# Routing tokens to experts: five chunks instead of six, and a new order of the steps inside a chunk

## The reference, cut to what matters

```
x  = x + gnn(...)                       # h of the last batch norm is added
xn = layernorm(layernorm(x))            # the expert block normalises twice
logits = layernorm(x) @ Wr + br         # [6250, 8]
top_p, top_idx = top_k(softmax(logits), 2)
weights = top_p / top_p.sum()
out = sum over the 2 experts of weights * (gelu(xn_e @ W1[e] + b1[e]) @ W2[e] + b2[e])
```

## Time and profile before

| what | us |
|---|---|
| median of three runs (5987.56 to 5988.58) | 5987.89 |
| the profiled execution's own time | 5985.42 |
| its span, first to last instruction | 5983.6 |
| `route()`, first instruction to that of `experts()` | 3373.6 to 3558.6 |
| mean granted TensorE clock, share of full speed | 0.758 |

### The profile page before, as it was taken

One profiled execution on the slowest core, in us unless ns is written; L12 is line 12 of the kernel. 1 busy time (PEld: TensorE's weight loads), 2 busy tenths in 40 slices (PEclk: granted clock), 3 DMA queues, 4 the chain that ended last, 5 costly groups with the idle time before them and its releaser, 6 DMA issues. The chain is left out here.

```text
span 5983.6 us, 101443 instructions
## 1 busy us (share of the span) xinstructions
PE 4448.4 (74%) x24203; PEld 3115.8 (52%) x24204; DVE 3008.1 (50%) x7622; ACT 2469.0 (41%) x6463; POOL 3450.6 (58%) x3585
## 2 busy tenths in 40 slices
PE   5477777767777776667667649999957777777898
PEld 4254545433444443334333449999945555555566
DVE  7544444444444444333333533333358778878745
ACT  0544444434344443333333324444444444444221
POOL 0477777777777776777777452222237776766001
PEclk6577777766666666666666659999978888888899
DMA  4677777767777776777777552222144443333101
GB/s 128 192 198 196 197 197 196 198 183 201 206 201 204 203 201 185 192 196 192 196 192 196 161 181 35 35 37 35 34 145 115 114 108 106 106 106 96 56 1 43
DMA packets 550732, 862.18 MB, mean 144 GB/s; under 512 B 210941, under 2 KB 398326, under 8 KB 550422
## 3 DMA queue, kind: packets, MB, share of 16 engines
q0 software_dynamic: 219840, 641.37, 40.5%
q1 hardware_dynamic: 330710, 218.97, 12.3%
HBM read 709.79 MB, written 150.21 MB: 144 GB/s over the span
## 5 line engine op out<-in xcount | busy, mean ns | idle before, releaser
L1024 POOL DMA_INDIRECT rows<-node_limbs,psrc x2496 | 2366.0, 948 | 832.2 <-issue 567.0
L1299 PE MATMUL ps<-rows,hot 128*128 128x257 bf16 x7488 | 1638.0, 365 | 874.4 <-DMA rows<-node_limbs,psrc 728.6
L1088 DVE TENSOR_TENSOR shared<-shared,ps 128x257 f32 x2496 | 1056.4, 423 | 1639.5 <-PE ps L1299 1332.1
L1299 PEld LDWEIGHTS ps<-rows,hot 128*128 128x128 bf16 x7488 | 772.0, 122 | 1673.4 <-DVE shared L1088 825.4
L2234 POOL DMA_INDIRECT rows<-attn_table,psrc x832 | 789.8, 949 | 385.7 <-issue 222.7
L1213 ACT ACTIVATE away<-iota_f,pdl 128x128 f32<-128x128 f32 x2496 | 759.2, 387 | 46.5 <-PE ps L1299 46.2
L2541 PE MATMUL ps<-rows,hot 128*128 128x264 f32 x1664 | 583.1, 500 | 231.8 <-DVE rows L2335 175.7
L2541 PEld LDWEIGHTS ps<-rows,hot 128*128 128x128 f32 x1664 | 370.8, 239 | 362.1 <-issue 174.0
L1870 POOL DMA_INDIRECT resid<-feat,slot_node x105 | 164.1, 1563 | 622.4 <-DVE feat L1885 619.6
L2356 DVE TENSOR_TENSOR sums<-sums,ps 128x264 f32 x832 | 356.8, 429 | 113.1 <-PE ps L2541 42.5
L1987 PEld LDWEIGHTS ps<-feat 128*128 128x128 f32 x3360 | 393.2, 193 | 8.3 <-DVE feat L1914 2.4
(11 more groups left out here) (466 smaller groups left out, 5298.8 us busy)
## 6 DMA issues: line engine op xcount, KB each, us to landing
slot_rows<-blank SPq DMA_DIRECT2D x450, 130.0 KB
rows<-node_limbs,psrc POOLq DMA_INDIRECT x2496, 3.3
feat<-in_edge_attr_dram SPq DMA_DIRECT2D x832, 32.0 KB
node_limbs<-limbs SPq DMA_DIRECT2D x99, 196.0 KB, 3.9
feat<-slot_rows SPq DMA_DIRECT2D x105, 130.0 KB
rows<-attn_table,psrc POOLq DMA_INDIRECT x832
node_limbs<-limbs SPq DMA_DIRECT2D x12, 784.0 KB, 3.6
w<-in_L_ffn_W_dram SPq DMA_DIRECT2D x8, 1024.0 KB, 11.6
```

The lines of the kernel that those rows point to most:

```text
L1024: g.indirect_dma_start(rows[:, n % RING, :], None, tables[k % 2], bass.IndirectOffsetOnAxis(ap=psrc[:, n:n + 1], axis=0)).then_inc(row_sem ...
L1088: v.tensor_tensor(row, row, ps[banks(k, i)[h * G + b]][:, 0:F + 1], ALU.add).then_inc(added.h, 1)
L1299: mm = pe.matmul(ps[cycle[s]][:, 0:F + 1], hot[:, 2 * half + h, b, :], rows[:, s, m * LIMB:m * LIMB + F + 1], start=(m == 0), stop=(m == 2))
```

## The change: what it does

The chunks become five: 7, 9, 11, 11 and 11 tiles. `picks(n - 1)` follows right after `spreads(n)`, so one chunk later instead of two. `ranks(n - 2)` moves to after the fourth addition of chunk n. ACT normalises four tiles, then does `second(n - 1)`, and stays four tiles ahead of its copies. PE does `rank(n - 2)` after the second tile of a chunk, and awaits the router's weights after the first tile of chunk 1; DVE awaits them before its first picks.

```
-        CHUNKS = [(0, 4), (4, 9), (9, 17), (17, 27), (27, 38), (38, NT)]
+        CHUNKS = [(0, 7), (7, 16), (16, 27), (27, 38), (38, NT)]
+        SOME = 4
 # DVE
-                    v.wait_ge(wr_in.h, 32)
-                    for n in range(len(CHUNKS) + 2):
-                        lo, hi = CHUNKS[n] if n <= LAST else (0, 0)
+                    for n, (lo, hi) in enumerate(CHUNKS):
                         for d in range(lo, hi):
                             add(d)
                             if d > lo:
                                 seen(d - 1)
-                            if n > 1 and d == lo + 4:
-                                picks(n - 2)
-                        if n <= LAST:
-                            seen(hi - 1)
-                            spreads(n)
-                        else:
-                            picks(n - 2)
-                        if n > 1:
-                            ranks(n - 2)
+                            if n > 1 and d == lo + SOME - 1:
+                                ranks(n - 2)
+                        seen(hi - 1)
+                        spreads(n)
+                        if n == 1:
+                            v.wait_ge(wr_in.h, 32)
+                        if n > 0:
+                            picks(n - 1)
+                    ranks(LAST - 1)
+                    picks(LAST)
+                    ranks(LAST)
 # ACT
                         a.wait_ge(scale_ready.h, n + 1)
-                        expert_row(lo)
-                        for e in range(lo + 1, hi):
+                        for e in range(lo, lo + SOME):
                             expert_row(e)
-                            keep(e - 1)
-                            if n > 0 and e == min(lo + 5, hi - 1):
-                                second(n - 1)
-                        keep(hi - 1)
+                        if n > 0:
+                            second(n - 1)
+                        for e in range(lo, hi):
+                            if e + SOME < hi:
+                                expert_row(e + SOME)
+                            keep(e)
 # PE
-                    pe.wait_ge(wr_in.h, 32)
-                    for n in range(len(CHUNKS) + 2):
+                    for n in range(len(CHUNKS) + 1):
 ...
                         for d in range(lo, hi):
                             turn_hidden(d, n)
+                            if n == 1 and d == lo:
+                                pe.wait_ge(wr_in.h, 32)
                             if n > 1 and d == lo:
-                                logit(lo_before - 1, n - 2)
+                                logit(CHUNKS[n - 2][1] - 1, n - 2)
+                            if n > 1 and d == lo + 1:
+                                rank(n - 2)
                             if d - lo >= AHEAD - 1 and before:
                                 z_tile(before.pop(0))
-                            if n > 1 and d == min(lo + 7, hi - 1):
-                                rank(n - 2)
                         if n > LAST:
                             logit(CHUNKS[n - 2][1] - 1, n - 2)
-                            if n > LAST + 1:
+                        for at, e in enumerate(before):
+                            z_tile(e)
+                            if n > LAST and at == 1:
                                 rank(n - 2)
-                        for e in before:
-                            z_tile(e)
-                        if n == LAST + 1:
-                            rank(n - 2)
-                        lo_before = lo
+                    logit(NT - 1, LAST)
+                    rank(LAST)
```

More of the change, by code:

```diff
@@ L1768, in rank @@
                         pe.matmul(of_bank(P), ones[:], by_expert, start=True, stop=True).then_inc(ranked.h, 1)
-                    pe.wait_ge(wr_in.h, 32)
-                    for n in range(len(CHUNKS) + 2):
+                    for n in range(len(CHUNKS) + 1):
                         lo, hi = CHUNKS[n] if n <= LAST else (0, 0)
-                        before = list(range(*CHUNKS[n - 1])) if 0 < n <= LAST + 1 else []
+                        before = list(range(*CHUNKS[n - 1])) if n > 0 else []
                         late = before[:1]
```

## The result

The changed kernel takes 5973.0 us (median of ten runs, 5971.3 to 5978.2) against 5988.8 (ten, 5982.2 to 5992.6): a ratio of 0.9975, 95% interval 0.9967 to 0.9984. Forecast: 5974.7, a ratio of 0.9978. The profiled execution took 5974.99, its span 5973.2.

What follows compares the result with a forecast made beforehand. POOL's scatters, fed in chunks by DVE and PE, bound the stage: third chunk starts at 3458.0, plus 82.4 and 2 x 1.275, ends at 3542.9, 13.2 us less. Median 5987.89 becomes 5974.7, range 5968 to 5981.5.

Steps and rivals of the forecast that it cites:

- last scatter ends: POOL's end of the stage: 3458.0 + 82.4 + 2 x 1.275 = 3542.9, against 3556.1 before.
- What bounds the stage: In the routing stage, POOL alone ends it: 98 scatters need 125 us, plus 20.0 us of waits for slots between chunks.
- The cycle of 22.7 and 23.0: Chain of PE and DVE from one chunk's end of picks to the next: 22.7 or 23.0 us.
- the 0.94 between slots and POOL: For each chunk, POOL begins scattering 0.94 us after its slots are known, read from 3410.36 to 3411.30.
- The table load of Exp: On ACT, Exp with one table load has 2.9 us behind the picks and is in time.
- The moved waits: The two unconditional waits that moved cost nothing: bias row in by 3378 before, both now reached later.
- PE's earlier start: PE no longer stands 12.0 us for the bias row; it waits for `affine(0)` and begins at 3375.9.
- the low level: PE's granted clock in the chunks taken as 0.50 (1.2 GHz), giving a step of 1.60 us a tile.
- Rival 1: PE at 2.4 GHz in the chunks, DVE sets a cycle of 20.1: 19.7 us less, 5968.2; chance 0.15.
- Rival 2: Two cycles 3 us longer each, from instruction gaps and ACT's copy: 7 us less than before, 5981; chance 0.17.
- Rival 3: `logit` always late, PE's step 2.4 instead of 1.60: end 4 us later than before, 5992; chance 0.06.
- The sum: Whole stage: last scatter's end from 3556.1 to 3542.9, 13.2 us less.

Runs made afterwards that it cites:

- the table of four kernels: Kernel before, its five new chunks only, its new order only, and the changed kernel: last scatter ends 182.5, 178.9, 172.2 and 169.3 us after ACT's first `affine`.
- the third chip: The changed kernel measured again, unaltered, on a chip where the kernel before takes 6832.4 us: 6833.7 us, ratio 1.0002.
- the filled kernel: The changed kernel with PE's idle stretches filled with 26 and 18 transposes that nobody reads: 5970.3 us, ratio 0.9970 to the kernel before.
- even chunks: The changed kernel with six chunks of 7, 7, 8, 8, 9 and 10 tiles: 6819.1 us on the third chip, ratio 0.9980 to the kernel before.

## Why the prediction was right

Step by step, forecast and measured (absolute positions; the stage began 0.26 us earlier in the changed kernel's execution):

| step | forecast | measured |
|---|---|---|
| first addition | 3376.6 | 3376.32 |
| `picks(0)`, `(1)`, `(2)` end | 3404.9, 3427.6, 3450.6 | 3404.86, 3427.99, 3451.23 |
| POOL, first scatter | 3412.0 | 3411.90 |
| second chunk, wait | 3434.9, 5.1 | 3434.66, 5.12 |
| third chunk, wait | 3458.0, about 0.2 | 3458.13, 0.80 |
| last scatter ends | 3542.9 | 3542.69 |
| next stage behind it | 2.5 | 2.6 |
| last instruction of `ranks(3)`, `ranks(4)` | 3480, 3499 | 3480.4, 3498.7 |

DVE's rows at the ends of `picks` in the changed kernel:

```profile
3404.86 0.75 DVE L1510 TENSOR_TENSOR shared<-shared,ps 128x256 f32<-128x256 f32 x2
...
3427.99 0.75 DVE L1510 TENSOR_TENSOR shared<-shared,ps 128x256 f32<-128x256 f32 x2
...
3451.23 0.74 DVE L1510 TENSOR_TENSOR shared<-shared,ps 128x256 f32<-128x256 f32 x2
```

- What bounds the stage (POOL, fed in chunks by a chain of DVE and PE): right, and the table of four kernels shows that it holds for each half of the change alone.
- The cycle of 22.7 and 23.0: it was 23.1 and 23.2, 0.43 and 0.24 longer. `spreads(2)` took 5.19 instead of 4.70 and `picks(2)` 4.88 instead of 4.64, with gaps of 0.21 and 0.33 that the profile calls "issue".
- Some of the closeness is luck. `picks(2)` ended 0.63 late, but POOL's third chunk began only 0.13 late, because the 0.94 between slots and POOL was too long for it. That term was read at the first chunk, where it is 0.93 again; at the second and third it is 0.37 (`ranks(2)` ends at 3457.76, POOL begins at 3458.13). The kernel before shows the short one too: `ranks(3)` ends at 3473.40 and POOL goes on at 3473.76. The prediction overlooked it.

```profile
3457.67 0.18 DVE L1622 CAST slots<-w 128x22 int32<-128x22 f32 x1
```

- The table load of Exp: the forecast laid it behind the picks. ACT did it at 3402.67, ahead of its wait for them. It cost nothing either way.
- The moved waits "cost nothing", and PE's earlier start: confirmed alone at 2.5 us in the trace, though the times don't tell it from nothing.
- The clock: I took the low level, and it held where it counts. In 3432 to 3436 the changed kernel has PE busy 4.00 at 0.50; after 3454 it rises for a while (0.66 and 0.77 in the windows from 3452 and 3456), too late for the slots that bind. This was a choice between two levels that both stood in rows 8, and not derived: on the third chip the same kernel has 0.80 in 4042 to 4046, in its second cycle.

```profile
3432.00:3436.00 4.00, 4.00 (x22) 4.00 (x21) 3.56 (x16) 1.96 (x5) 1.04 (x2) 0.50 0.00 0
3452.00:3456.00 4.00, 4.00 (x27) 3.98 (x26) 3.11 (x13) 2.19 (x7) 3.09 (x4) 0.66 0.28 100
```

- Rival 1 needed a clock that stays up. It doesn't even in the filled kernel, which won 2 us of the 6.3. Rival 2's longer cycles did not come on this chip, and came on the others by another mechanism, one that I had not listed. Rival 3's step of 2.4 did not come either: it is 1.60, even with the copy made twice.
- The sum was 13.2. In the stage it is 13.2 from `affine` to the last scatter (182.5 and 169.3), in the medians 15.7, with an interval of 9.6 to 19.8. That the median came within 1.7 us of the forecast is closer than the interval can vouch for; the stage is what bears the forecast out.

The forecast holds for the chip it was made for. On the third chip the same kernel gains nothing, and I find no row in the trace before that could have told.

## What to carry to other kernels

Where one engine drains work that others make in chunks, its end is the start of its first chunk, plus its own work, plus its waits between chunks. Larger chunks mostly move time from the third term to the first (here a net 3.6 us), and a shorter chain from one chunk to the next lowers the sum (10.3). The sizes deserve the same working: even chunks won 14.6 us on the third chip, where this change won nothing. So write down, for each chunk, when it is ready and how much is left from there, and look at the largest. Put a wait behind whatever its engine can do without it: moving the two for the router's weights was worth 2.5 us of the stage.

## What the runs showed of the hardware that I had not expected

- The same kernel took 5988, 6777 and 6832 us on three chips. In `route()` of the changed kernel the instructions last as long on the third chip as on the first (a scatter 0.97, a PE step 1.60); what differs are pauses of PE, ACT and DVE at once, up to 8.6 us long in that trace, that begin where the writes of one queue and the indirect scatters of another run together. They are a small part of the difference: of the 847 us between the changed kernel's spans on these two chips, 603 lie ahead of `route()`, 43 in it and 201 behind it, and the rest was not looked into.
- PE went from 2.4 GHz to 1.2 after a wait of under 2 us and stayed there while it was busy without a pause (3412 to 3424 of the filled kernel), yet ran the same mix at 2.4 GHz from 3434 to 3440.
